# A graph-attention kernel: who weighs the third quarter of each batch, VectorE or ScalarE

## The reference, cut to what matters

```python
q = (x @ Wq + bq).reshape(n, H, C)
k = (x @ Wk + bk).reshape(n, H, C)
v = (x @ Wv + bv).reshape(n, H, C)
alpha = jnp.einsum('ehc,ehc->eh', q[dst], k[src]) / jnp.sqrt(jnp.float32(C))
amax = jax.ops.segment_max(alpha, dst, num_segments=n)
ex = jnp.exp(alpha - amax[dst])
denom = jax.ops.segment_sum(ex, dst, num_segments=n)
attn = ex / denom[dst]
msg = (v[src] * attn[:, :, None]).reshape(-1, H * C)
out = jax.ops.segment_sum(msg, dst, num_segments=n)
```

## Time and profile before

| | us |
|---|---|
| median of 3 runs | 2817.81 (2807.45 to 2825.65) |
| the profiled execution, its own time | 2806.19 |
| its span in the trace | 2804.5 |
| attention, first gather to last add | 256.6 to 968.6 |
| VectorE busy in the span | 1941.9 (69%) |
| TensorE busy (matmuls) | 2188.2 (78%) |
| ScalarE busy | 1399.9 (50%) |
| GpSimd busy | 1587.4 (57%) |

### The profile page before, as it was taken

One profiled execution on the slowest core, in us unless ns is written; L12 is line 12 of the kernel. 1 busy time (PEld: TensorE's weight loads), 2 busy tenths in 40 slices (PEclk: granted clock), 3 DMA queues, 4 the chain that ended last, 5 costly groups with the idle time before them and its releaser, 6 DMA issues. The chain is left out here.

```text
span 2804.5 us, 41419 instructions
## 1 busy us (share of the span) xinstructions
PE 2188.2 (78%) x11127; PEld 1471.0 (52%) x11128; DVE 1941.9 (69%) x4018; ACT 1399.9 (50%) x4455; POOL 1587.4 (57%) x1697
## 2 busy tenths in 40 slices
PE   6996777787777756869994687887777789999775
PEld 3554555555555545746651433333334677878663
DVE  4564899999999788720119799999997433332786
ACT  2221555666556534512124598999996422222242
POOL 2644766666666211567777677777775177777000
PEclk9997788888888775579996799999999689999997
DMA  3213766666676110314323333333331311111005
GB/s 110 59 46 105 219 205 205 198 197 198 206 208 197 47 62 11 114 30 129 94 75 86 116 105 104 104 105 104 104 104 49 83 39 40 40 39 40 9 1 196
DMA packets 167619, 292.87 MB, mean 104 GB/s; under 512 B 53832, under 2 KB 101965, under 8 KB 167398
## 3 DMA queue, kind: packets, MB, share of 16 engines
q0 software_dynamic: 77520, 186.78, 24.1%
q1 hardware_dynamic: 80720, 87.10, 9.9%
q10 hardware_dynamic: 9158, 16.33, 1.6%
HBM read 253.35 MB, written 36.75 MB: 103 GB/s over the span
## 5 line engine op out<-in xcount | busy, mean ns | idle before, releaser
L971 POOL DMA_INDIRECT at_kv<-kv_tab,e_src x440 | 431.7, 981 | 258.5 <-PE at_a L1093 143.1
L2447 PE MATMUL cv_ps<-cv_msg,cv_hot 128*128 128x512 f32 x880 | 417.3, 610 | 119.1 <-DVE acc L2509 90.2
L2434 POOL DMA_INDIRECT cv_x<-x_tab,e_src x440 | 424.6, 965 | 140.1 <-issue 91.4
L2465 ACT ACTIVATE cv_msg<-cv_x,factors 128x64 f32<-128x64 f32 x1320 | 358.1, 337 | 0.0
L2857 POOL DMA_INDIRECT gs_h<-h_tab,fc_q x280 | 264.5, 945 | 147.2 <-issue 79.2
L2447 PEld LDWEIGHTS cv_ps<-cv_msg,cv_hot 128*128 128x128 f32 x880 | 158.7, 192 | 341.8 <-ACT cv_msg L2465 172.7
L2025 POOL DMA_INDIRECT pairs<-gating_pair,gating_place x256 | 251.8, 984 | 125.7 <-issue 64.7
L2509 DVE TENSOR_TENSOR acc<-acc,cv_ps 128x256 f32 x880 | 307.8, 417 | 6.1 <-PE cv_ps L2447 4.7
L1093 PE MATMUL at_a<-at_kv,at_hot_e 128*128 128x264 f32 x880 | 254.9, 419 | 12.3 <-ACT at_hot_e L1020 8.2
L1068 PE MATMUL at_q<-q_parts,at_hot_n 128*128 x1320 | 230.0, 330 | 43.6 <-DVE at_kv L1165 21.9
L2462 ACT ACTIVATE cv_msg<-cv_x,factors 128x256 f32<-128x256 f32 x440 | 218.7, 497 | 17.9 <-DMA cv_x<-x_tab,e_src 17.9
(11 more groups left out here) (556 smaller groups left out, 4239.4 us busy)
## 6 DMA issues: line engine op xcount, KB each, us to landing
x_space<-in_L_ffn_w SPq DMA_DIRECT2D x16, 1024.0 KB, 7.0
at_rel_row<-e_rel_rows SPq DMA_DIRECT2D x55, 256.0 KB, 4.2
experts_out<-gs_y ACTq DMA_DIRECT2D x20, 512.0 KB
x_y<-experts_out SPq DMA_DIRECT2D x20, 512.0 KB, 7.4
at_kv<-kv_tab,e_src POOLq DMA_INDIRECT x440, 4.0
cv_x<-x_tab,e_src POOLq DMA_INDIRECT x440, 2.7
kv_tab<-p_qkv SPq DMA_DIRECT2D x25, 256.0 KB, 2.0
gs_h<-h_tab,fc_q POOLq DMA_INDIRECT x280, 2.4
```

The costliest lines, as they stand in the source:

```text
L971: nc.gpsimd.indirect_dma_start(out=kv[:, t % (RING * Q4), 0:2 * D], out_offset=None, in_=kv_tab, in_offset=bass.IndirectOffsetOnAxis(ap=e. ...
L2434: nc.gpsimd.indirect_dma_start(out=xg[:, i % RT, u, :], out_offset=None, in_=x_tab, in_offset=bass.IndirectOffsetOnAxis(ap=e.src[:, t:t + ...
L2447: nc.tensor.matmul(ps[u % R][:, :], hot[:, i % 2, u, :], msg[:, i % 2, u, :], start=True, stop=True).then_inc(summed, 1)
L2465: ins = nc.scalar.activation(parts[:, 1, 1 + m], xg[:, i % RT, u, 0:M], ACT.Copy, scale=factor[:, t:t + 1, 1 + m])
```

## The change

ScalarE's `weigh` goes, with its semaphore `at_weighed`. VectorE's `weight` is called for the third quarter too, ahead of the add of duo 4; the weighing of the fourth quarter now stands behind that add. TensorE waits for the one semaphore `at_weighted` throughout, which now counts every half.

```diff
-        weighed, reached = s.sem("at_weighed"), s.sem("at_reached")
+        reached = s.sem("at_reached")
...
-                def weigh(j, us):
-                    hh = 4 * j + 2
-                    if hh >= halves:
-                        return
-                    act.wait_ge(exped, hh + 1)
-                    for u in us:
-                        for h in range(H1):
-                            row = kv[:, hh % RING * Q4 + u, D + h * HD:D + (h + 1) * HD]
-                            ins = a(row, row, ACT.Copy, scale=kv[:, hh % RING * Q4 + u, 2 * D + h:2 * D + h + 1])
-                        ins.then_inc(weighed, 1)
-
...
                     edge_hot(4 * j + 1)
-                    weigh(j, (0, 1))
-                    weigh(j, (2, 3))
                     edge_hot(4 * j + 2)
...
                         pe.wait_ge(built, p // 2 + 1)
-                        if p // 2 % 4 == 2:
-                            pe.wait_ge(weighed, Q4 * (p // 8 + 1))
-                        else:
-                            pe.wait_ge(weighted, p // 8 * 3 + (0, 1, 0, 2)[p // 2 % 4] + 1)
+                        pe.wait_ge(weighted, p // 2 + 1)
...
                     add(i, 3)
                     multiply(at + 5)
+                    weight(A, 2)
+                    add(i, 4)
                     weight(A, 3)
-                    add(i, 4)
                     reduce(S, 2)
                     add(i, 5)
```

## The result

The changed kernel takes 2871.89 us (median of 4 runs, 2866.88 to 2878.78) against 2814.14 us before (4 runs, 2807.45 to 2825.65): a ratio of 1.0207 with a 95% interval of 1.0178 to 1.0237, or 50 to 67 us more. The profiled execution takes 2869.09 us with a span of 2867.4 us, 62.9 us more than the span before. The forecast was 2880 (2848 to 2906), and 63 us against the profile.

The account below looks back on a forecast made before the run. The prediction took VectorE's queue as the bound. +2.44 us a batch over 25 batches (61.0), plus 1.3 and 0.7 at the ends, gave 63.0 us: 2869 against the profile, 2881 by the median, taken as 2880, range 2848 to 2906.

Parts of the forecast that it names:

- What bounds the kernel: In attention, VectorE's queue sets the pace, busy 92.39 of 100 us; ScalarE idles 8.6 us a batch waiting for it.
- Removed: ScalarE's 32 copies weighing the third quarter go; this gives back 0.22 us a batch, at the add of duo 4.
- Added: One 128x1024 product a batch on VectorE, weighing the third quarter, costs its queue 1.14 us.
- Moved: Third quarter's weighing directly precedes the add of duo 4: 2.66 us from start to start, 1.44 idle.
- The sum: +2.44 us a batch over 25 batches, 61.0 us, plus 1.3 in the first and 0.7 in the last full one: 63.0.
- Half from the product, half from the wait: Of the 63.0 us in attention, about half was to come from VectorE's added product and half from its wait.
- The bounds at A0 to A2: VectorE's waits at the adds of duos 0 to 2, 0.77 us a batch: no change, bounds -21 to +21 us.
- The first rival: TensorE's clock falls a second time in each batch, slowing duo 4's sum: +25 us, 2906 by the median; 10%.
- The second rival: Something covers duo 4's sum, so only the product's 31 us remain: 2849 us by the median; 4%.
- the third: Late one-hots from ScalarE cause VectorE's waits for TensorE; removing them leaves +4 us, 2822 by the median; 4%.
- A miss among the signs: ScalarE's wait for VectorE's `at_fall` was to grow from 8.6 to some 18 us a batch.

Follow-up runs that it names:

- act_behind: Kernel before, ScalarE still weighing the third quarter, with only VectorE's weighing of the fourth moved behind the add of duo 4: 2839.2 us, ratio 1.0099.
- split: Kernel before with second and third quarters' one-hots a pass sooner and ScalarE also weighing two of the fourth quarter's four tiles: 2784.2 us, ratio 0.9903.
- early_hot: Kernel before with ScalarE's one-hot of each batch's second quarter made at the end of the pass before: 2792.6 us, ratio 0.9945.
- cover: The change with the third quarter weighed two places sooner and the fourth quarter's weighing ahead of the add of duo 4: 2827.1 us, ratio 1.0055.
- sliver: The change with the third quarter's product cut to one feature per head (128x32), leaving part of the computation out: 2848.9 us, ratio 1.0141.
- halved: The change with the third quarter weighed by two 128x512 products, TensorE told after each: 2871.0 us, ratio 1.0214.
- warm_after: The change with TensorE kept at products of zeros in five idle places of each batch: 2851.1 us, ratio 1.0149 to the kernel before.
- warm_halved: The change with the third quarter weighed in two halves and TensorE kept at products of zeros in its idle gaps: 2840.7 us, ratio 1.0112.

## Why the prediction was right

- **What bounds the kernel.** VectorE's queue: act_behind adds no work and costs 28 us; split takes work off VectorE and puts it on ScalarE and gains.
- **Removed: worth 0.22 us a batch, at A4 only.** Right for the change: A4 is now released by VectorE. As a statement on ScalarE's lateness it was too small: early_hot took 0.60 us off a batch, since its batches also met the clock sooner, at A0.
- **Added: 1.14 us of queue.** W3 to the next start in the change is 602.80 - 601.67 = 1.13 us; 110 products with a mean of 1217 ns.
- **Moved: 2.66 us from W2 to A4.** 2.64 measured, idle 1.42 (forecast 1.44), in every batch. cover and sliver show from two sides that it is this order and not the product.
- **The sum.** +2.44 us a batch forecast, 27.29 - 24.89 = 2.40 measured; 63.0 us in all, 62.0 from first add to last and 62.9 in the span. The 25 batches between cost 59.8 us (61.0 forecast). The first costs 1.5 us from its first add to the wide rescaling behind it, and the last full one 1.0, a little more than the +1.3 and +0.7 forecast; the last half batch gives 0.3 back.
- **Half from the product, half from the wait.** This was bookkeeping, not cause. Taken in one sequence, the product with its sum covered costs 15.5 us (cover) and the order then 45; in the other, the order alone costs 28 us (act_behind) and the product then 30 to 33. So neither part has a price of its own: the product is partly paid by waits that go with it.
- **The bounds at A0 to A2.** The three waits together stayed at 0.83 us a batch (0.82 before), so the middle value was right, but by luck rather than by the reason given ("the work ahead of A0 keeps its order"). The three waits together are 1.26 us in halved, 0.57 in early_hot and 0.22 in warm_after and warm_halved, with VectorE's work ahead of A0 unchanged.
- **The first rival**, 10%, did not come in the change (1.13 us for duo 4's sum) but did in warm_after. It was nearer than 2.16 us of idle time without a fall made it look. The Trainium skill (TensorE: Matmul & The Clock Gate, HAM oscillation) describes bursts of matmuls that start at the lower clock after a wait; in warm_after the trace agrees, with 2.09 us for the duo against 1.13. The waits in that section's case are for DMA and longer than those here, so the prediction read too much into it when it called this rival the likelier case by it.
- **The second rival** is what cover makes true, by moving two lines, and at 2827 us where the rival had 2849 by the median; **the third** asked for one-hots that cost VectorE 1.14 us a batch. early_hot took their lateness away and won 0.60. The lateness itself was 0.23 of that, close to TensorE's own waits (0.2 us a batch); with what came along with it, half of the rival's price was there and not a fifth.
- **A miss among the signs.** ScalarE's wait for `at_fall` was to grow to 18 us a batch; it is 336.6 / 20.5 = 16.4. The other 38.7 / 20.5 = 1.9 us it now waits for TensorE, ahead of the fourth quarter's one-hot: with three buffers it is too early.

## What to carry to other kernels

When a step is moved between engines, look at the two instructions on either side of its new place. The step ahead of a consumer should not be the one whose result another engine must first work on; any other piece of the queue that is long enough covers the round trip, here 1.42 us each time, for free. An engine that waits in every round for the bound engine is the one to give work to, not to take it from, and a saving in one place of a round has to be read in the whole round, since the clock can give or take as much at another.

## What the runs showed of the hardware that was not expected

The moment at which TensorE's clock comes back up in a batch can outweigh what was saved: 0.53 us saved from W2 to A4 left 0.04 us a batch (halved), and 0.23 us saved at A4 came with 0.25 more at A0 (early_hot).

A product of two SBUF operands on VectorE holds up GpSimd's gathers. GpSimd's timeline in the changed kernel, around W2 (625.70 to 626.92) and W3 (628.96 to 630.18):

```profile
624.60 0.94 POOL L971 DMA_INDIRECT at_kv<-kv_tab,e_src  x1 [0.30 <-DVE at_kv L1149]
625.85 1.89 POOL L971 DMA_INDIRECT at_kv<-kv_tab,e_src  x1 [0.30 <-DVE at_kv L1149]
628.04 0.95 POOL L971 DMA_INDIRECT at_kv<-kv_tab,e_src  x1 [0.30 <-PE at_a L1077]
629.29 1.71 POOL L971 DMA_INDIRECT at_kv<-kv_tab,e_src  x1 [0.30 <-PE at_a L1077]
```

The two that begin under a product take 1.89 and 1.71 us instead of 0.95. In the change 55 gathers begin under a product, and all of them end 0.81 to 0.83 us behind that product's end: the sooner one begins, the longer it takes, from 1.96 us down to 1.17. What VectorE does in the same time otherwise changes nothing. Gathers that begin under a reduction of the same length, with one SBUF input, or under a product or an add with one input in PSUM, take at most 0.96 us. Gathers longer than 1.3 us number 54 in the change and 15 before, and in the batch of sliver shown above only the one under W3 (645.04, 1.71 us) is long. The Trainium skill (SBUF — State Buffer, Who interferes with whom) says that a VectorE instruction with two SBUF inputs contends with GpSimd instructions that read SBUF, and the trace agrees. The same section infers that a `tensor_tensor` does not hold up an indirect DMA's descriptors; for these gathers the measurement decides. It cost nothing here: from 292 us on no VectorE instruction of the attention waits for a gather, in either kernel.
